# Shifted-window transformer block: the attention loop of the matmul engine regrouped, y finished in three parts, x loaded behind y's store

## The chip, the cores and the metric

The kernel runs on one core of a Trainium2 chip. The core has five engines with a program each: TensorE (PE, matmuls; PEld is its weight load), VectorE (DVE), ScalarE (ACT), GpSimd (POOL) and SyncE (SP), which here issues nearly all DMAs. They wait for one another by semaphores. The metric is the device time of one execution in microseconds (us), the median of several runs.

## The reference, cut to what matters

```python
x: (32, 56, 56, 128)   # windows 7 x 7, shift 3, 16 heads of 8, hidden 512
y   = roll(layernorm(x) * g1 + b1, (-3, -3))           # cut into 8 x 8 windows of 49 tokens
q, k, v = split(y @ qkv_w.T + qkv_b)
a   = softmax(q * 8 ** -0.5 @ k.T + rel_bias + mask)    # 49 x 49 for each window and head
o   = (a @ v) @ proj_w.T + proj_b
x1  = x + roll(o, (3, 3))
h   = gelu((layernorm(x1) * g2 + b2) @ fc1_w.T + fc1_b)
out = x1 + h @ fc2_w.T + fc2_b
```

## The kernel before

A step works on one band: seven image rows of two images, 16 windows in 8 pairs w = 0 to 7. There are 128 steps, and a software pipeline of turns t = -2 to 130 (`turns`, `body`): turn t runs the attention of step t, the row maxima of step t+1 (max_logits on PE, `row_maxima` on DVE), the projection and second norm of step t-1 and the two-layer perceptron (fc1, gelu, fc2) of step t-2, and loads x of step t+3. Each engine's program is written out in the order in which it runs; nothing is scheduled by a planner. PE, DVE and ACT are strictly in the order of the code, with semaphores between them.

In a turn PE first does the **front**: pv of the last window quartet of step t-1, `TZ` (transposes of z, L853), `TX` (of x, L861), the transpose of the maxima (L758), the rest of the fc2 rows of step t-3 (L832, L837), fc1 chunks 0 and 1 (L814), the q and k projections (L882), fc1 chunks 2 and 3, the spreading of the reciprocals of the softmax sums (L896), v (L910) and the output projection (L919). Then comes the **loop** over w. I call its pieces L (logits of a window pair, L780 and L785), M (max_logits, L750), P (pv of two window pairs, L800) and F (fc2 of one of seven rows i, 8 matmuls L832 and 4 L837). The loop before is L0 L1 M0 F M1 L2 P0 M2 L3 F M3 L4 P1 M4 L5 F M5 L6 P2 M6 L7 F M7, and P3 opens the next front. fc2 rows 3 to 6 are done in the loop (part 1 of `FC2_PARTS`), rows 0 to 2 in the front of the next turn (part 0).

What one piece waits for: M(w) waits until DVE has taken the maxima of M(w-1) (s_max), since both use banks 0 and 1. L(w) waits for the exp of w-2 on ACT (two pairs of banks), P(u) for the exps of its two pairs and for ACT's copy of P(u-1). fc2 writes bank 7. `finish` (L569, DVE) adds the scaled fc2 rows to x1_b and writes y_out; SP stores y_out when both parts are finished (s_fin). The F rows of a turn also need hid_hi (DVE, L578 and L580) and hid_lo (POOL, L375).

DVE in the loop takes the maxima of M(w) (L587) and in each gap some statistics: of x1 at w = 0 to 2, the aggregate (L512) at w = 3, of x_in of step t+3 (L506) at w = 4 to 6, after s_x says that it has landed. Behind the loop come `finish` of part 1 and the moments of x_in. In the front DVE does, in order: h_lo, neg_maxT, yT_lo, the reciprocal (L628), `finish` of part 0, hid_hi 0 and 1, k_lo and q_lo (L639), oT (L655), hid_hi 2 and 3, v, x. ACT does in the front h_hi, yT_hi, a table load, gelu 0 and 1 (L421), k_hi and q_hi (L467), gelu 2 and 3, a table load and copies of v; in the loop the exps (L406) and the copies of P (L414).

SP issues in a turn, in this order: sums out of pv_sb (L235), the load of x_in for step t+3 (L186), oT_raw (L248), the negated maxima (L224), r_rows (L261: the split reciprocals, for L896), mx_k and mx_q (L273, L277), the store of y_out (L186), fifteen copies for st_k and st_q (L292, L295) and the load of x_res (L186). The loads of x_in and x_res, the store and oT_raw are two DMAs of 196 KB each, r_rows two of 24.5 KB. Before it issues one it waits on its semaphores, and all that stands behind waits too.

Of the kernel before, what the change touches and what calls it, by code (L numbers as in the profile page):

```python
# [38 lines left out]
FC2_PARTS = ((0, 3), (3, 7))  # L39
# [10 lines left out]
def swin_block_kernel(nc, x, wqT, wkT, wvT, wvpT, wpT, w1T, w2T, cols, rows, table_k, table_q, ident, eye,  # L50
# [11 lines left out]
    with ctx:  # L62
# [134 lines left out]
        def _(sp):  # L197
# [29 lines left out]
            def body(t, edge, odd):  # L227
# [8 lines left out]
                n = t + 3  # L236
                if exists(n):

                    sp.wait_ge(s_st1, n)
                    if past(n, 1):  # L240
                        sp.wait_ge(s_t1, n - 1)
                    band_dmas(sp, xr, x_in[odd(3)], n, edge(n), False, s_x)
# [67 lines left out]
        def _(pool):  # L310
# [31 lines left out]
            def body(t, edge, odd):  # L342
# [22 lines left out]
                if exists(n):  # L365
                    if past(n, 0):
                        pool.wait_ge(s_fin, 2 * n)
# [20 lines left out]
        def _(act):  # L388
# [35 lines left out]
            def body(t, edge, odd):  # L424
# [59 lines left out]
                if exists(t):  # L484
                    for w in range(NW):
# [3 lines left out]
                        if w % 2 == 0 and w > 0:  # L489
                            copy_pv(t, w // 2 - 1)  # L490

# [4 lines left out]
        def _(dve):  # L496
# [64 lines left out]
            def finish(n, p, edge):  # L561

                i0, i1 = FC2_PARTS[p]
                if p == 1:
                    dve.wait_ge(s_x1b, n + 1)
                    if past(n, 0):
                        dve.wait_ge(s_stored, loads(n - 1, edge(n) and edge(n - 1)))
                dve.wait_ge(s_fc2, 2 * n + 2 - p)
                nc.vector.scalar_tensor_tensor(  # L569
                    y_out[:, i0:i1, :], ps[0:TP, 7, 0:(i1 - i0) * C].rearrange("p (i c) -> p i c", c=C),  # L570
                    1 / W_SCALE, x1_b[:, i0:i1, :], ALU.mult, ALU.add).then_inc(s_fin, 1)

            def hid_high(n, c):
                dve.wait_ge(s_gelu, CH * n + c + 1)
                if c == 0 and past(n, 0):
                    dve.wait_ge(s_fc2, 2 * n)
# [16 lines left out]
            def body(t, edge, odd):  # L593
# [35 lines left out]
                if exists(t - 3):  # L629
                    finish(t - 3, 0, edge)  # L630
# [54 lines left out]
                for w in range(NW):  # L685
# [3 lines left out]
                    if exists(n):  # L689
# [5 lines left out]
                        if w == 3:  # L695
                            aggregate(n, st2, s_st2, mv2, s_ln2)
                    n = t + 3
                    if exists(n):

                        if w == 4:  # L700
                            dve.wait_ge(s_x, loads(n, edge(n)))
                            stats(x_in[odd(3)], st1, (0, 1))
                        if w == 5:
                            stats(x_in[odd(3)], st1, (1, 4))
                        if w == 6:
                            stats(x_in[odd(3)], st1, (4, WS)).then_inc(s_st1, 1)
                if exists(t - 2):
                    finish(t - 2, 1, edge)
# [6 lines left out]
        def _(pe):  # L715
# [102 lines left out]
            def fc2(n, p, i):  # L818
                first, end = FC2_PARTS[p]
                if i == first and p == 1:  # L820
# [4 lines left out]
                    elif n > 0:  # L825
                        pe.wait_ge(s_fin, 2 * n)
                if i == first and p == 0:
                    pe.wait_ge(s_fin, 2 * n + 1)
                row = ps[0:TP, 7, (i - first) * C:(i - first + 1) * C]
# [4 lines left out]
                for c in range(CH):  # L834
                    if i == first and p == 1:
# [5 lines left out]
            def body(t, edge, odd):  # L841
# [30 lines left out]
                if exists(n):  # L872
                    pe.wait_ge(s_y_lo, n + 1)
                    high, low = ([y[odd(1)][:, :, im, 0:WT] for im in range(2)] for y in (yT_hi, yT_lo))
                    for w_hi, w_lo, bank in ((wk_hi, wk_lo, 0), (wq_hi, wq_lo, 6)):
                        if bank == 6 and exists(t):
                            pe.wait_ge(s_negT, t + 1)
                        if bank == 6 and exists(t - 3):
                            pe.wait_ge(s_fin, 2 * (t - 3) + 2)
# [20 lines left out]
                if exists(n):  # L900
                    if exists(t + 1):
                        pe.wait_ge(s_lo, 2 * (t + 2))
                    else:
                        pe.wait_ge(s_negT, t + 1)
                        if exists(t - 3):
                            pe.wait_ge(s_fin, 2 * (t - 3) + 2)
# [14 lines left out]
                for w in range(NW):  # L921
                    if exists(t):
                        if w != 1:
                            logits(t, w, edge, odd(0))
                        if w == 0:
                            logits(t, 1, edge, odd(0))
                        if w % 2 == 0 and w > 0:
                            pv(t, w // 2 - 1)
                    if exists(t - 2) and w % 2:
                        fc2(t - 2, 1, FC2_PARTS[1][0] + w // 2)  # L930
                    if exists(t + 1):
                        max_logits(t + 1, w, edge)
# [64 lines left out]
```

## Time and profile before

| | us |
|---|---|
| runs of the kernel before | 3899.22, 3900.76, 3903.62 (median 3900.76) |
| the profiled execution, its own time | 3904.86 |
| its span, first to last instruction | 3903.1 |
| PE busy in it | 3744.1 (96%) |
| DVE busy | 3087.1 (79%) |
| POOL busy | 2884.4 (74%) |
| ACT busy | 2776.0 (71%) |
| mean granted clock of TensorE, share of full speed | 0.993 |

The busy time of PE counts modelled ends of pipelined matmuls, so its idle time is best read between the starts of instructions. The span is divided by 128 steps: from one output projection (L919) to the next PE takes between 29.24 and some 30.6 us in the steady part, half of the turns below 29.42, 29.51 in the mean of 124 turns. Idle time of the other engines costs only where PE, or a chain that PE waits for, stands behind it.

### The profile page before, as it was taken

The page shows a single profiled execution, that of the slowest core. Times are in us where ns is not written, and L with a number is a line of the kernel's source. Part 1 is how long each engine was busy: PE and PEld are TensorE (multiplying, and loading weights), DVE is VectorE, ACT ScalarE, POOL GpSimd, SP SyncE. Part 2 cuts the span into 40 slices and gives each one's busy share as a digit, 9 for nine tenths or more (in the row PEclk, how much of TensorE's full clock was granted, in tenths as well). Part 3 has the DMA queues.
Part 4 walks back from the last instruction along what each step waited for, and adds up shares of the span by engine and source line. Part 5 has one row for each costly group of instructions (what it writes and reads, how often), then busy time and mean ns, then how long its engine had stood idle before and what let it go on. Part 6 is the DMA issues. An engine that isn't in the chain of part 4 may idle for free. (4 is left out here: it accounts for less than half of the span.)

```text
span 3903.1 us, 176619 instructions
## 1 busy us (share of the span) xinstructions
PE 3744.1 (96%) x75664; PEld 2946.8 (76%) x75664; DVE 3087.1 (79%) x7840; ACT 2776.0 (71%) x3840; POOL 2884.4 (74%) x3988
## 2 busy tenths in 40 slices
PE   2899999999999999999999999999999999999997
PEld 1677777777777777777777777777777777777776
DVE  6788878878878878878887888888888788888874
ACT  1677777777777777777777777777777777777774
POOL 5577777777777777777777777777777777777775
PEclk8999999999999999999999999999999999999999
DMA  2343334434434434433433344333344334333331
GB/s 76 106 119 118 115 112 118 119 111 116 121 114 115 118 115 118 117 115 115 118 117 111 115 119 116 114 117 116 111 118 120 112 116 119 115 115 117 117 108 58
DMA packets 603457, 441.97 MB, mean 113 GB/s; under 512 B 135939, under 2 KB 602227, under 8 KB 602675
## 3 DMA queue, kind: packets, MB, share of 16 engines
q1 hardware_dynamic: 602211, 428.86, 37.2%
q8 instruction: 597, 9.78, 1.1%
q14 instruction: 185, 1.52, 0.1%
q0 software_dynamic: 464, 1.81, 0.1%
HBM read 106.14 MB, written 51.46 MB: 40 GB/s over the span
## 5 line engine op out<-in xcount | busy, mean ns | idle before, releaser
L587 DVE TENSOR_REDUCE neg_max<-ps 113x16 f32<-113x784 f32 x1024 | 999.6, 976 | 545.5 <-PE ps L750 439.1
L406 ACT ACTIVATE probs<-ps 113x784 f32<-113x784 f32 x1024 | 848.1, 828 | 656.9 <-PE ps L785 539.5
L375 POOL TENSOR_TENSOR hid_lo<-probs,hid_hi 128x784 f16<-128x784 f32 x512 | 881.3, 1743 | 76.6 <-DVE hid_hi L580 76.3
L785 PE MATMUL ps<-st_q,st_k 128*49 128x196 f16 x8192 | 694.5, 249 | 0.0
L780 PE MATMUL ps<-bias,eye_k 106*64 106x392 f16 x4096 | 684.3, 331 | 0.0
L750 PE MATMUL ps<-mx_k,mx_q 128*49 128x196 f16 x8192 | 541.6, 253 | 60.3 <-DVE neg_max L587 52.4
L785 PEld LDWEIGHTS ps<-st_q,st_k 128*49 128x49 f16 x8192 | 440.2, 105 | 125.4 <-issue 0.5
L421 ACT ACTIVATE probs<-ps,col 128x784 f32<-128x784 f32 x512 | 467.6, 913 | 89.5 <-PE ps L814 60.1
L832 PE MATMUL ps<-w_hi,hid_hi 128*112 128x128 f16 x3584 | 521.7, 226 | 3.8 <-DVE hid_hi L580 3.0
L832 PE MATMUL ps<-w_lo,hid_hi 128*112 128x128 f16 x3584 | 498.8, 220 | 0.0
L832 PEld LDWEIGHTS ps<-w_hi,hid_hi 128*112 128x112 f16 x3584 | 417.7, 130 | 83.8 <-issue 79.4
L800 PE MATMUL ps<-probs,v_own 113*32 113x49 f32 x32768 | 470.3, 209 | 8.3 <-issue 7.6
L800 PEld LDWEIGHTS ps<-probs,v_own 113*32 113x32 f32 x32768 | 397.1, 110 | 92.3 <-issue 90.9
L750 PEld LDWEIGHTS ps<-mx_k,mx_q 128*49 128x49 f16 x8192 | 317.3, 103 | 137.6 <-DVE neg_max L587 74.4
L832 PEld LDWEIGHTS ps<-w_lo,hid_hi 128*112 128x112 f16 x3584 | 419.1, 131 | 0.0
L338 POOL TENSOR_SCALAR x_in<-x_in,rs,nm 112x128 f32<-112x128 f32 x896 | 389.4, 450 | 13.5 <-POOL nm L333 0.4
L338 POOL TENSOR_SCALAR z<-x,rs,nm 112x128 f32<-112x128 f32 x896 | 388.7, 450 | 13.5 <-POOL nm L333 0.4
L329 POOL TENSOR_TENSOR rs<-ve,half 112x7 f32<-112x7 f32 x256 | 380.4, 1486 | 21.3
L414 ACT ACTIVATE pv_sb<-ps 128x392 f32<-128x392 f32 x512 | 255.2, 498 | 182.0 <-PE ps L800 171.4
L356 POOL TENSOR_SCALAR r_hi<-sums 128x98 f16<-128x98 f32 x128 | 36.4, 284 | 461.3 <-DVE sums L628 461.3
L350 POOL TENSOR_TENSOR x_res<-x_res,proj_b 112x896 f32<-112x896 f32 x128 | 268.9, 2101 | 131.2 <-DMA x_res<-in_x 131.1
L837 PE MATMUL ps<-w_hi,hid_lo 128*112 128x128 f16 x3584 | 349.3, 220 | 3.4 <-POOL hid_lo L375 3.4
(119 smaller groups left out, 8009.9 us busy)
## 6 DMA issues: line engine op xcount, KB each, us to landing
st_k<-k_hi SPq DMA_DIRECT2D x256, 196.0 KB
st_q<-q_hi SPq DMA_DIRECT2D x1024, 49.0 KB
oT_raw<-pv_sb SPq DMA_DIRECT2D x256, 196.0 KB, 3.8
x_in<-in_x SPq DMA_DIRECT2D x224, 196.0 KB
x_res<-in_x SPq DMA_DIRECT2D x224, 196.0 KB
out_y<-y_out SPq DMA_DIRECT2D x224, 196.0 KB
mx_k<-k_hi SPq DMA_DIRECT2D x512, 49.0 KB
mx_q<-q_hi SPq DMA_DIRECT2D x128, 196.0 KB
```

The costliest lines, as they stand in the source:

```text
L329: nc.gpsimd.tensor_tensor(rs[:, :], ve[:, :], half[:, :], ALU.pow).then_inc(s_rs, 1)
L338: last = nc.gpsimd.tensor_scalar(z[:, i, :], src[:, i, :], rs[:, i:i + 1], nm[:, i:i + 1], ALU.mult, ALU.add)
L375: nc.gpsimd.tensor_tensor(hid_lo[:, c, :], hid[:, c, :], hid_hi[:, c, :], ALU.subtract).then_inc(s_hid_lo, 1)
L406: nc.scalar.activation(probs[0:KP, w % 4, :].rearrange("p (b c) -> p b c", b=2), ps[0:KP, b:b + 2, 0:HB * WT], ACT.Exp).then_inc(s_exp, 1)
L421: nc.scalar.activation(hid[:, c, :].rearrange("p (b q) -> p b q", b=2), ps[:, bank:bank + 2, 0:HT], ACT.Gelu, bias=col[:, BF + c:BF + c + ...
L587: nc.vector.tensor_reduce(neg_max[0:KP, :, :, w].rearrange("p e g -> p g e"), ps[0:KP, 0:2, :].rearrange("p b (g c) -> p (b g) c", g=2)[:, ...
L750: last = mm(group(im, 0, g, 256), mx_q[edge(n)][:, g, span], mx_k[:, g, :, span], start=True, stop=True)
L780: mm(ps[HP * im:HP * (im + 1), bank + b, 0:HB * WT], eye_k[0:BIAS_ROWS, kind, im, :], bias[0:BIAS_ROWS, b, :], start=True, stop=False)
L785: last = mm(group(im, bank, g, EQ * WT), st_k[par][:, g, span], st_q[par][:, :, g, span], start=False, stop=(g % 2 == 1))
L800: last = mm(ps[32 * r:32 * r + VC, 6, first:first + WT], v_own[0:KP, w, h, :], probs[0:KP, w % 4, h * WT:(h + 1) * WT], start=True, stop=True)
L832: mm(row, hid_hi[:, c, i * TP:(i + 1) * TP], w_part[:, c, :], start=(c == 0 and w_part is w2_hi), stop=False)
L837: last = mm(row, hid_lo[:, c, i * TP:(i + 1) * TP], w2_hi[:, c, :], start=False, stop=(c == CH - 1))
```

## The change

1. **fc2 rows.** `FC2_PARTS` becomes rows 0-1, 2-3 and 4-6. Five rows (0 to 4) are done in the loop and two (5 and 6) in the front. Part p may start when part p-1 is finished, for p > 0.
2. **The loop of PE** is written out: L0 L1 M0 F0 F1 M1 L2 P0 M2 L3 L4 M3 P1 L5 M4 F2 F3 M5 L6 L7 M6 P2 F4 M7. fc2 rows stand in twos at two places, and the logits L3 L4 and L6 L7 follow each other.
3. **finish** (DVE): parts 0 and 1 (two rows each) after the maxima of w = 3 and w = 5, part 2 (three rows) where part 0 stood in the front; the one behind the loop is gone. Of the statistics of x_in three rows stand at w = 4 and one at w = 5, where it was one and three.
4. **ACT** copies P2 behind the exp of w = 7, which was behind the exp of w = 6.
5. **SP** loads x_in behind the store of y_out.

```diff
-FC2_PARTS = ((0, 3), (3, 7))
+FC2_PARTS = ((0, 2), (2, 4), (4, 7))
+FC2_BANK = (0, 2, 0)
+PARTS = len(FC2_PARTS)
...
@@ block.sync: x_in (of step t+3) was issued ahead of oT_raw, now behind this @@
                 n = t - 3
                 if exists(n):
-                    sp.wait_ge(s_fin, 2 * (n + 1))
+                    sp.wait_ge(s_fin, PARTS * (n + 1))
                     band_dmas(sp, outr, y_out, n, edge(n), True, s_stored)
+                n = t + 3
+                if exists(n):
+
+                    sp.wait_ge(s_st1, n)
+                    if past(n, 1):
+                        sp.wait_ge(s_t1, n - 1)
+                    band_dmas(sp, xr, x_in[odd(3)], n, edge(n), False, s_x)
...
-                        if w % 2 == 0 and w > 0:
+                        if w in (2, 4):
                             copy_pv(t, w // 2 - 1)
+                    copy_pv(t, NU - 2)
...
@@ finish @@
-                if p == 1:
+                if p == 0:
...
-                dve.wait_ge(s_fc2, 2 * n + 2 - p)
+                dve.wait_ge(s_fc2, PARTS * n + p + 1)
...
@@ fc2 @@
-                if i == first and p == 0:
-                    pe.wait_ge(s_fin, 2 * n + 1)
+                if i == first and p > 0:
+                    pe.wait_ge(s_fin, PARTS * n + p)
...
@@ front of PE @@
                 if exists(t - 3):
-                    for i in range(*FC2_PARTS[0]):
-                        fc2(t - 3, 0, i)
+                    fc2(t - 3, 5)
+                    fc2(t - 3, 6)
```

In what follows, three places in the order of the instructions. On PE in the middle of the loop, before: F, M3, L4, P1, M4, L5 (L837 is the end of an fc2 row, L750 M, L780 and L785 L, L800 P).

```order
L837 MATMUL ps<-w_hi,hid_lo 112x128 x4
L750 MATMUL ps<-mx_k,mx_q 49x196 x8
L780 MATMUL ps<-bias,eye_k 64x392 x2
L785 MATMUL ps<-st_q,st_k 49x196 x4
L780 MATMUL ps<-bias,eye_k 64x392 x2
L785 MATMUL ps<-st_q,st_k 49x196 x4
L800 MATMUL ps<-probs,v_own 32x49 x32
L750 MATMUL ps<-mx_k,mx_q 49x196 x8
L780 MATMUL ps<-bias,eye_k 64x392 x2
L785 MATMUL ps<-st_q,st_k 49x196 x4
L780 MATMUL ps<-bias,eye_k 64x392 x2
L785 MATMUL ps<-st_q,st_k 49x196 x4
```

The same place in the changed kernel, where the lines are L756 for M, L786 and L791 for L and L806 for P: M2, L3 and L4, M3, P1.

```order
L756 MATMUL ps<-mx_k,mx_q 49x196 x8
L786 MATMUL ps<-bias,eye_k 64x392 x2
L791 MATMUL ps<-st_q,st_k 49x196 x4
L786 MATMUL ps<-bias,eye_k 64x392 x2
L791 MATMUL ps<-st_q,st_k 49x196 x4
L786 MATMUL ps<-bias,eye_k 64x392 x2
L791 MATMUL ps<-st_q,st_k 49x196 x4
L786 MATMUL ps<-bias,eye_k 64x392 x2
L791 MATMUL ps<-st_q,st_k 49x196 x4
L756 MATMUL ps<-mx_k,mx_q 49x196 x8
L806 MATMUL ps<-probs,v_own 32x49 x32
```

The fc2 row that stood between L3 and M3 is gone, and L4 has moved ahead of M3.

On DVE in the same loop, from the maxima of w = 3 (L587 is neg_max) to the moments behind the loop, before:

```order
L587 TENSOR_REDUCE neg_max<-ps 113x4x4
L512 BN_AGGR mv<-st 112x2 x7
L587 TENSOR_REDUCE neg_max<-ps 113x4x4
L506 BN_STATS st<-x_in 112x6
L587 TENSOR_REDUCE neg_max<-ps 113x4x4
L506 BN_STATS st<-x_in 112x6 x3
L587 TENSOR_REDUCE neg_max<-ps 113x4x4
L506 BN_STATS st<-x_in 112x6 x3
L587 TENSOR_REDUCE neg_max<-ps 113x4x4
L569 SCALAR_TENSOR_TENSOR y_out<-ps,x_b 112x512
L512 BN_AGGR mv<-st 112x2 x7
```

And now, where L591 is neg_max and L573 finish:

```order
L591 TENSOR_REDUCE neg_max<-ps 113x4x4
L515 BN_AGGR mv<-st 112x2 x7
L573 SCALAR_TENSOR_TENSOR y_out<-ps,x_b 112x256
L591 TENSOR_REDUCE neg_max<-ps 113x4x4
L509 BN_STATS st<-x_in 112x6 x3
L591 TENSOR_REDUCE neg_max<-ps 113x4x4
L573 SCALAR_TENSOR_TENSOR y_out<-ps,x_b 112x256
L509 BN_STATS st<-x_in 112x6
L591 TENSOR_REDUCE neg_max<-ps 113x4x4
L509 BN_STATS st<-x_in 112x6 x3
L591 TENSOR_REDUCE neg_max<-ps 113x4x4
L515 BN_AGGR mv<-st 112x2 x7
```

finish of four rows behind the loop has become two of two rows, after the maxima of w = 3 and of w = 5.

On SP, from the copy of the sums to the first st_k, before (L186 with x_in is the load of x, with out_y the store):

```order
L235 DMA sums<-pv_sb 128x1x49 x2
L186 DMA x_in<-in_x 56x7x128 x2
L248 DMA oT_raw<-pv_sb 128x1x392 x2
L224 DMA st_q<-neg_maxT 1x128x98
L261 DMA r_rows<-r_hi 16x8x98
L261 DMA r_rows<-r_lo 16x8x98
L273 DMA mx_k<-k_hi 8x4x784 x4
L277 DMA mx_q<-q_hi 32x4x784
L186 DMA out_y<-y_out 56x7x128 x2
L292 DMA st_k<-k_hi 32x4x784
```

And now (L188 for both):

```order
L237 DMA sums<-pv_sb 128x1x49 x2
L243 DMA oT_raw<-pv_sb 128x1x392 x2
L226 DMA st_q<-neg_maxT 1x128x98
L256 DMA r_rows<-r_hi 16x8x98
L256 DMA r_rows<-r_lo 16x8x98
L268 DMA mx_k<-k_hi 8x4x784 x4
L272 DMA mx_q<-q_hi 32x4x784
L188 DMA out_y<-y_out 56x7x128 x2
L188 DMA x_in<-in_x 56x7x128 x2
L294 DMA st_k<-k_hi 32x4x784
```

The load of x_in no longer stands ahead of oT_raw, the maxima and r_rows, but behind the store of y and ahead of the st copies and x_res.

## Rows read from the trace of the kernel before

**Rows 1.** Waits of PE: engine line <- releaser: us in total, times, longest us

```profile
PE ps L750 <- DVE neg_max L587: 52.4, 140, 1.1
...
PE ps L896 <- DMA r_rows<-r_lo: 8.1, 14, 1.9
```

**Rows 2.** PE in order of time, a loop: start us, duration us, engine line [idle before]

```profile
1743.49 0.36 PE L780 MATMUL ps<-bias,eye_k 106*64 106x392 f16 x2
...
1744.88 0.51 PE L750 MATMUL ps<-mx_k,mx_q 128*49 128x196 f16 x8
1745.32 0.26 PE L832 MATMUL ps<-w_hi,hid_hi 128*112 128x128 f16 x1
...
1746.52 0.53 PE L750 MATMUL ps<-mx_k,mx_q 128*49 128x196 f16 x8 [0.32 <-DVE neg_max L587]
...
1748.49 0.53 PE L750 MATMUL ps<-mx_k,mx_q 128*49 128x196 f16 x8
1748.86 0.33 PE L780 MATMUL ps<-bias,eye_k 106*64 106x392 f16 x2
...
1749.64 0.26 PE L832 MATMUL ps<-w_hi,hid_hi 128*112 128x128 f16 x1
...
1750.44 0.53 PE L750 MATMUL ps<-mx_k,mx_q 128*49 128x196 f16 x8
```

**Rows 3.** PE in order of time, the front that follows that loop

```profile
1758.29 0.53 PE L750 MATMUL ps<-mx_k,mx_q 128*49 128x196 f16 x8
1758.75 0.90 PE L800 MATMUL ps<-probs,v_own 113*32 113x49 f32 x64
1759.58 0.89 PE L853 MATMUL ps<-idn,z 112*128 112x112 f32 x7
...
1761.75 0.22 PE L832 MATMUL ps<-w_hi,hid_hi 128*112 128x128 f16 x1
...
1763.09 0.49 PE L814 MATMUL ps<-h_hi,w_hi 128*128 128x392 f16 x2
...
1769.21 0.50 PE L896 MATMUL ps<-r_rows,sel 32*128 32x392 f16 x2
1769.64 0.23 PE L910 MATMUL ps<-wv_hi,yT_hi 128*128 128x128 f16 x1
...
1771.02 1.24 PE L919 MATMUL ps<-w_p,oT 128*112 128x128 f32 x9
```

**Rows 4.** ACT in order of time, same turns: exp of w=3, gelu, k_hi

```profile
1749.80 0.82 ACT L406 ACTIVATE probs<-ps 113x784 f32<-113x784 f32 x1 [0.56 <-PE ps L785]
...
1764.29 1.91 ACT L421 ACTIVATE probs<-ps,col 128x784 f32<-128x784 f32 x2 [0.43 <-PE ps L814]
1766.38 0.93 ACT L467 ACTIVATE k_hi<-ps,col 128x784 f16<-128x784 f32 x1 [0.19 <-PE ps L882]
```

**Rows 5.** DVE in order of time, same turns: maxima of w=3, aggregate, finish, q_lo

```profile
1751.02 0.98 DVE L587 TENSOR_REDUCE neg_max<-ps 113x16 f32<-113x784 f32 x1 [0.39 <-PE ps L750]
1751.91 0.57 DVE L512 BATCH_NORM_AGGREGATE mv<-st 112x2 f32<-112x6 f32 x7
...
1764.23 0.49 DVE L569 SCALAR_TENSOR_TENSOR y_out<-ps,x_b 112x384 f32<-112x384 f32 x1
...
1768.42 1.15 DVE L639 SCALAR_TENSOR_TENSOR q_lo<-ps,col,q_hi 128x392 f16<-128x392 f32 x2
```

**Rows 6.** SP in order of time, same turns: DMA issues and their durations

```profile
1741.74 1.12 SPq L186 DMA_DIRECT2D out_y<-y_out  x2
...
1761.61 1.00 SPq L186 DMA_DIRECT2D x_in<-in_x  x2
...
1766.28 0.62 SPq L261 DMA_DIRECT2D r_rows<-r_lo  x1
```

**Rows 7.** DMAs of tile r_rows, whole run: us from issue to landing

```profile
DMA to landing us min/median/max: 2.0/2.5/3.4
```

**Rows 8.** The same, window 3770 to 3800 us, where no x is loaded

```profile
DMA to landing us min/median/max: 2.0/2.0/2.0
```

More of the change, by code:

```diff
@@ L629, in body @@
                 if exists(t - 3):
-                    finish(t - 3, 0, edge)
+                    finish(t - 3, 2, edge)
                 if exists(t - 2):
@@ L696, in body @@
                             aggregate(n, st2, s_st2, mv2, s_ln2)
+                    if exists(t - 2) and w == 3:
+                        finish(t - 2, 0, edge)
+                    if exists(t - 2) and w == 5:
+                        finish(t - 2, 1, edge)
                     n = t + 3
@@ L816, in fc1, with fc2 @@
                 last.then_inc(s_fc1, 1)
-            def fc2(n, p, i):
+            def fc2(n, i):
+                p = next(k for k, (first, end) in enumerate(FC2_PARTS) if first <= i < end)
                 first, end = FC2_PARTS[p]
-                if i == first and p == 1:
+                if i == 0:
                     pe.wait_ge(s_hid_hi, CH * (n + 1))
@@ L825, in fc2 @@
                     elif n > 0:
-                        pe.wait_ge(s_fin, 2 * n)
-                if i == first and p == 0:
-                    pe.wait_ge(s_fin, 2 * n + 1)
-                row = ps[0:TP, 7, (i - first) * C:(i - first + 1) * C]
+                        pe.wait_ge(s_fin, PARTS * n)
+                if i == first and p > 0:
+                    pe.wait_ge(s_fin, PARTS * n + p)
+                place = FC2_BANK[p] + i - first
+                row = ps[0:TP, 7, place * C:(place + 1) * C]
                 for c in range(CH):
@@ L834, in fc2 @@
                 for c in range(CH):
-                    if i == first and p == 1:
+                    if i == 0:
                         pe.wait_ge(s_hid_lo, CH * n + c + 1)
@@ L920, in body @@
                         last.then_inc(s_proj, 1)
[L921 to L932, printed above, removed]
+                now, mlp, ahead = exists(t), exists(t - 2), exists(t + 1)
+                if now:
+                    logits(t, 0, edge, odd(0))
+                    logits(t, 1, edge, odd(0))
+                if ahead:
+                    max_logits(t + 1, 0, edge)
+                if mlp:
+                    fc2(t - 2, 0)
+                    fc2(t - 2, 1)
+                if ahead:
+                    max_logits(t + 1, 1, edge)
+                if now:
+                    logits(t, 2, edge, odd(0))
+                    pv(t, 0)
+                if ahead:
+                    max_logits(t + 1, 2, edge)
+                if now:
+                    logits(t, 3, edge, odd(0))
+                    logits(t, 4, edge, odd(0))
+                if ahead:
+                    max_logits(t + 1, 3, edge)
+                if now:
+                    pv(t, 1)
+                    logits(t, 5, edge, odd(0))
+                if ahead:
+                    max_logits(t + 1, 4, edge)
+                if mlp:
+                    fc2(t - 2, 2)
+                    fc2(t - 2, 3)
+                if ahead:
+                    max_logits(t + 1, 5, edge)
+                if now:
+                    logits(t, 6, edge, odd(0))
+                    logits(t, 7, edge, odd(0))
+                if ahead:
+                    max_logits(t + 1, 6, edge)
+                if now:
+                    pv(t, 2)
+                if mlp:
+                    fc2(t - 2, 4)
+                if ahead:
+                    max_logits(t + 1, 7, edge)
             turns(body)
```

23 lines of the change are left out of this document (8 added, 15 removed).

## The prediction

> **What bounds the kernel now.** I read the busy shares first, then the waits, then one turn in order of time on each engine. TensorE (PE) is the engine that hardly stops; DVE, ACT and POOL wait for it more than it waits for them. So a turn costs what PE's pieces cost from start to start, plus its few waits. By name these are small: 52.4 us for M behind DVE's maxima, 8.1 us for the spreading of the reciprocals behind the DMA of r_rows [rows 1]. In the turn of [rows 2, 3] the first appears once, 0.32 us ahead of M1. From the first logits (1743.49) to P3 (1758.75) the loop takes 15.26 us, from TZ (1759.58) to the projection (1771.02) the front takes 11.44 us.
>
> Second, each piece costs more when its neighbour is of another kind. An fc2 row between strangers takes 0.80 us up to the next M (1749.64 to 1750.44), a row beside rows 0.67 (two rows from 1761.75 to 1763.09) [rows 2, 3]. M ahead of L takes 0.37 (1748.49 to 1748.86), ahead of F or P 0.44 to 0.46 (1744.88 to 1745.32; 1758.29 to 1758.75). L ahead of F takes 0.78, two L ahead of M together 1.39, so some 0.70 each. P takes 0.83 [rows 2, 3].
>
> Third, the front is a chain on several engines which PE only just does not wait for. The projection needs oT (DVE), that needs the spread reciprocals and q_lo; v needs q_lo, which ends at 1768.42 + 1.15 = 1769.57, and v starts at 1769.64 [rows 3, 5]. r_rows is issued at 1766.28, and the median landing is 2.5 us, so it is there at 1768.78, 0.43 ahead of the use at 1769.21 [rows 3, 6, 7]. Whatever PE saves here is worth only as much as these two give way.
>
> **Part 1, the loop.** The new loop in pieces: L0 L1 to M0 1.39; M0 0.44; F0 F1 0.67 + 0.80 = 1.47; M1 0.37; L2 0.78; P0 0.83; M2 0.37; L3 L4 1.39; M3 0.46; P1 0.83; L5 0.70; M4 0.46; F2 F3 1.47; M5 0.37; L6 L7 1.39; M6 0.46; P2 0.83; F4 0.80; M7 0.46. The sum is 15.27 us, against 15.26 now: the fifth fc2 row (0.67) comes in at no cost, because the stall ahead of M1 goes (0.4) and three fc2 groups instead of four change over (0.2). P ahead of L or F is not in the trace; P ahead of TZ is 0.83, I take that, and the dearest changeover seen, 0.14, is the upper bound: 2 x 0.14 a turn, 35 us for all. The lower one is nothing.
>
> Do new waits arise? M(w) can follow M(w-1) by what M1 does now, 1746.52 - 1744.88 = 1.64. The new distances are 1.91, 1.98, 1.76, 1.99, 1.93, 1.76, 2.09: all above. On DVE the widest slot is w = 3: the maxima start 0.58 after M3, the aggregate 0.89 later, it lasts 0.57, and then comes the new finish of two rows; three rows take 0.49 [rows 2, 5]. With 0.34 to 0.49 for two, y's first part is ready 2.4 to 2.55 us after M3, and F2, which now waits for it, is due 0.46 + 0.83 + 0.70 + 0.46 = 2.45 after M3. So 0 to 0.15 us; I take 0, since two rows must be shorter than three and an instruction starts a little before its forerunner's end (0.89 for 0.98). P1 needs the exp of w = 3: it starts 0.94 after L3 (1748.86, 1749.80) and lasts 0.82, so it ends 1.76 after L3, and P1 is due at 1.39 + 0.46 = 1.85 [rows 2, 4]. Copying P2 behind the exp of w = 7 costs nothing: P3 needs the copy 2.1 us after P2's start, where exp and copy are through. The finish that left the space behind the loop ends a piece of DVE time in which it then waits for ACT anyway: nothing gained.
>
> **Part 2, the front.** PE does two fc2 rows instead of three: 0.67 us less from TZ on. What of it arrives?
> - ACT waited 0.43 ahead of gelu and 0.19 ahead of k_hi, both for PE [rows 4]. With PE 0.67 earlier both waits vanish, and the chain gelu, k_hi, k_lo, q_lo comes 0.6 us earlier, no more, for then ACT is full. So v can start 0.6 earlier.
> - r_rows is needed at 1769.21 - 0.67 = 1768.54; at a landing time of 2.5 us it is late by 0.24.
>
> So I put the front at 0.60 less, if r_rows lands within 2.2 us.
>
> **Part 3, the move of x.** The load of x (196 KB twice) stands now between the sums and oT_raw on SP and takes its place in the rings ahead of r_rows (1761.61, r_rows 1766.28) [rows 6]. In the four last turns no x is loaded, with all else in place: there r_rows lands in 2.0 us each time, against 2.5 median and 3.4 at most over the run [rows 7, 8]. The new order is that of those turns. So r_rows is there at 1768.28, ahead of 1768.54. The waits of the tail, some 3 of the 8.1 us [rows 1], go too.
> What stands behind x on SP now comes about 1.0 us later (1.00 is its issue time): fifteen st copies, needed in the next turn only, and x_res, needed by POOL half a turn later; I price both at nothing. x itself is issued at about 1742.9 (behind the store of 1741.74 and 1.12) and is read behind the maxima of w = 4, some 3.5 us after M3 at 1750.44: 11 us for it [rows 2, 6].
> The Trainium skill says in "DMA: Bandwidth & Descriptors", section Rules for kernel authors, that a DMA should be issued early and waited for late. That rule speaks against moving x back by nearly half a turn. Its own result is the third rival below; no row here shows x being waited for in either place.
>
> **Sum.** A turn: loop +0.01, front -0.60, so -0.59; over 125 turns with all parts in them -74 us, with the tail of r_rows -77. The profiled execution took 3904.86 us, so it would take 3828; against the median of the runs, 3900.76, that is 3824.
> The changeover can be weighed against a page. In this trace it costs: 0.80 against 0.67 for F, 0.46 against 0.37 for M. The Trainium skill ("TensorE: Matmul & The Clock Gate", Part 2, step by step) says that PE pulls a weight load ahead of running matmuls when row groups do not conflict or the background buffer is free; by that a changeover would be hidden, and grouping would bring 0.4 for the stall alone and not 0.6, 25 us less. The measured rows decide for 0.6.
>
> **Rivals.**
> - **r_rows stays at 2.5 us**, since oT_raw (the same size as x, twice) is still ahead of it. For: oT_raw is issued earlier but as close. Against: [rows 8]. Then the front gives 0.67 - 0.24 = 0.43, with the spread to 3.4 about 0.40, and the turn 0.39: 49 us, 3852.
> - **A small new wait in the loop**: F2 behind finish by up to 0.15, or P1 behind exp, where only 0.09 is left. At 0.12 a turn 15 us are lost: 3839. For: both are near. Against: they are on the right side.
> - **x comes too late (slower)**: DVE stands at w = 4 in front of s_x, the maxima of w = 5 behind it, and M6 of PE behind these. It decides from a landing time of 11 us on, and becomes a loss over the whole once that is 11.7, for a turn has 0.6 to give. At 12.1 us the loss is 0.4 a turn: 50 us, 3950. For: store and load, 784 KB, now follow each other, with the st copies behind. Against: the longest landing time in the rows, that of the small r_rows, is 3.4 us; a large transfer would have to take over three times that.
> - **Nothing gained**: another operand of the front (h_lo for fc1, x for M0) is as late as it is now relative to P3, so that PE saves 0.67 and waits 0.6. Then 3899. For: the front is tight everywhere. Against: in the turn shown PE has no wait in it except changeovers, and ACT's waits for PE show that PE was the later one.
>
> **How the numbers follow.** Forecast 0.62 (3808 to 3834), r_rows 0.15, a small wait 0.14, x late 0.04, nothing gained 0.05. The likeliest gives 3824. The range, 3806 to 3856, holds the first three: below, 0.67 in the front and all waits behind DVE and r_rows gone (95 us); above, the r_rows case. Within 0.2% (7.8 us, about what a measurement of this kernel can tell from no change) only "nothing gained": 0.04, with 0.01 of it and the x case on the slow side. Faster 0.91, same 0.04, slower 0.05.
>
> **What the profile would show.** Right: M behind neg_max is under 10 us in the waits of PE; L0 to P3 takes 15.3 us with five fc2 rows in it, TZ to the projection 10.8; r_rows lands in 2.0 to 2.2 us. ACT's waits of 0.43 and 0.19 ahead of gelu and k_hi are close to 0, which is the sign that the front is at its end. Wrong would be: PE waiting at L904 for r_rows by more than 0.1 a turn (first rival), fc2 behind y_out or pv behind probs (second), DVE's statistics of x_in behind DMA (third).

## The result: 0.64% slower, and the profile after

| us | before | after |
|---|---|---|
| runs, same chip | 3899.22 to 3903.62, median 3901.45 (4) | 3924.51 to 3929.18, median 3925.34 (4) |
| ratio after to before | | 1.0064, 95% interval 1.0052 to 1.0077 |
| span of the profiled execution | 3903.1 | 3922.7 |
| mean granted clock | 0.993 | 0.994 |
| PE busy | 3744.1 (96%) | 3723.3 (95%) |
| DVE busy | 3087.1 (79%) | 3149.5 (80%) |

The prediction was 3824. PE did shed 21 us of modelled busy time, DVE gained 62, and the whole became longer. The second table cuts a turn of PE from projection to projection, mean start to start over the 122 to 124 turns in which every piece is recorded; the last column adds the waits of PE that the profile puts down to "issue", over the whole run. M0 is the first max_logits of a loop, P3 the last pv, SPR the spreading of the reciprocals, PR the projection.

| us a turn | PR, L0, L1 | M0 to P3 | P3 | TZ to SPR | SPR to PR | turn | "issue", us in all |
|---|---|---|---|---|---|---|---|
| before | 3.15 | 13.90 | 0.94 | 9.70 | 1.82 | 29.51 | 8.5 |
| after | 3.67 | 13.96 | 1.14 | 9.09 | 1.82 | 29.68 | 40.8 |

The front came out as forecast: 0.61 less from TZ on. The loop carries its fifth fc2 row at 0.06. What ate the gain stands in two columns: 0.52 ahead of M0 and 0.20 at P3. Together +0.17 a turn, 21 us over 124 turns, against 19.6 in the spans. The waits of PE in the changed kernel (engine line <- releaser: us in all, times, longest) name both, and answer to [rows 1]:

```profile
PE ps L756 <- DVE x L686: 47.8, 115, 0.6
PE ps L806 <- issue: 34.1, 42, 1.9
...
PE ps L756 <- DVE neg_max L591: 12.3, 13, 1.1
PE ps L904 <- DMA r_rows<-r_lo: 7.7, 16, 1.6
```

The same two waits before:

```profile
PE ps L800 <- issue: 7.6, 19, 1.1
...
PE ps L750 <- DVE x L682: 3.3, 8, 0.6
```

M behind the maxima fell from 52.4 to 12.3, a little above the 10 foreseen.

**Where the 0.6 went.** The end of the front in the kernel before, in order of time (start us, duration us, [idle before]): DVE, then POOL, then the start of M0 on PE. L655 is oT, L580 the pair of casts hid_hi 2 and 3, L682 the add that makes x; L375 is hid_lo, two and two.

```profile
1769.80 1.16 DVE L655 TENSOR_TENSOR oT<-oT_raw,ps 128x343 f32<-128x343 f32 x4 [0.23 <-issue]
1770.88 1.03 DVE L580 CAST hid_hi<-probs 128x784 f16<-128x784 f32 x2
1771.84 1.06 DVE L673 COPY v_own<-ps 49x512 f32<-49x512 f32 x1
1772.75 1.13 DVE L682 TENSOR_TENSOR x<-ps,x_res 112x512 f32<-112x512 f32 x2
...
1765.61 2.09 POOL L368 TENSOR_TENSOR x_b<-x,fc_b 112x896 f32<-112x896 f32 x1
1767.66 3.30 POOL L375 TENSOR_TENSOR hid_lo<-probs,hid_hi 128x784 f16<-128x784 f32 x2
...
1774.12 0.51 PE L750 MATMUL ps<-mx_k,mx_q 128*49 128x196 f16 x8
```

The same place in the changed kernel, a turn whose TZ starts at 2012.92 (before: 1759.58):

```profile
2022.47 1.17 DVE L659 TENSOR_TENSOR oT<-oT_raw,ps 128x343 f32<-128x343 f32 x4 [0.23 <-issue]
2023.55 1.66 DVE L584 CAST hid_hi<-probs 128x784 f16<-128x784 f32 x2
2025.14 1.09 DVE L677 COPY v_own<-ps 49x512 f32<-49x512 f32 x1
2026.07 1.14 DVE L686 TENSOR_TENSOR x<-ps,x_res 112x512 f32<-112x512 f32 x2
...
2018.96 2.09 POOL L370 TENSOR_TENSOR x_b<-x,fc_b 112x896 f32<-112x896 f32 x1
2021.01 3.31 POOL L377 TENSOR_TENSOR hid_lo<-probs,hid_hi 128x784 f16<-128x784 f32 x2
...
2027.36 0.53 PE L756 MATMUL ps<-mx_k,mx_q 128*49 128x196 f16 x8 [0.39 <-DVE x L686]
```

Count from TZ. oT starts at 10.22 before and at 9.55 now, the casts at 11.30 and 10.63: DVE's chain is 0.67 earlier, as said. POOL's x_b starts at 6.03 and 6.04: it hangs on the reciprocal (L628 at 1763.56, L632 at 2016.90: 3.98 after TZ both times), which stands ahead of the shortened fc2 rows and so gained nothing. POOL's first hid_lo pair ended at 1770.96, 0.08 after the casts began; now it ends at 2024.32, 0.77 after. And the casts take 1.66 us instead of 1.03. The 0.63 is what DVE had won: x starts at 13.17 and 13.15. PE is there 0.6 earlier and waits for it.

In both kernels the length of that pair of casts follows the time t for which POOL still runs after its start: 1.04 for t under 0.1 (106 turns of before), 1.66 for t about 0.8 (84 turns of after), 1.86 to 1.87 for t about 1.0 (4 turns of before, 25 of after). So it is about t + 0.9 from t = 0.2 on, as if the first cast waited for POOL's end. Nine turns of before, with t from 0.7 to 1.0, had already shown the price (1.59 to 1.87).

The Trainium skill has the rule, which I had not weighed: "SBUF — State Buffer", section Who interferes with whom, says that casts of DVE can take a pair of SBUF ports that GpSimd uses too, that whoever issues first holds it for the whole instruction while the other blocks, and that tensor_reduce on trn2 never takes it. The trace agrees on the cast (1.03 against 1.66); the reduce is tried below.

**Other lines of after.** ACT in the same turn, for [rows 4]: gelu 0 and 1 without a wait (0.43 before), k_hi at 6.14 after TZ (6.80 before) with the same 0.19.

```profile
2017.10 1.76 ACT L423 ACTIVATE probs<-ps,col 128x784 f32<-128x784 f32 x2
2019.06 0.93 ACT L469 ACTIVATE k_hi<-ps,col 128x784 f16<-128x784 f32 x1 [0.19 <-PE ps L890]
```

Landing of r_rows over the run, for [rows 7], which has 2.0/2.5/3.4 for the kernel before:

```profile
DMA to landing us min/median/max: 2.0/2.0/2.8
```

DVE behind the maxima of w = 3 in the loop ahead, for [rows 5]: finish of two rows takes 0.40.

```profile
2004.77 0.57 DVE L515 BATCH_NORM_AGGREGATE mv<-st 112x2 f32<-112x6 f32 x7
2005.25 0.40 DVE L573 SCALAR_TENSOR_TENSOR y_out<-ps,x_b 112x256 f32<-112x256 f32 x1
```

**The stalls in P3.** Of the 42 waits of L806 (pv) for "issue", 32 stand in P3, with 30.3 of the 34.1 us (18 and 7.2 us before). Five of them in a row of time (PE; x is how many of the 64 matmuls are left behind the gap, the bracket is the gap):

```profile
1213.57 0.39 PE L806 MATMUL ps<-probs,v_own 113*32 113x49 f32 x17 [1.52 <-issue]
1302.37 0.38 PE L806 MATMUL ps<-probs,v_own 113*32 113x49 f32 x16 [0.72 <-issue]
1391.71 0.38 PE L806 MATMUL ps<-probs,v_own 113*32 113x49 f32 x15 [1.24 <-issue]
1480.57 0.38 PE L806 MATMUL ps<-probs,v_own 113*32 113x49 f32 x14 [0.63 <-issue]
1569.69 0.37 PE L806 MATMUL ps<-probs,v_own 113*32 113x49 f32 x13 [1.23 <-issue]
```

They are 89 us apart, three turns, and each comes one matmul later in the program than the one before. Nothing that the program waits for moves like that. It is a place in the stream of instructions, at a distance of almost exactly three turns' worth, at which PE runs dry.

The trace shows what PE waits for there. Queue 8 carries instructions, here packets and MB of the changed kernel:

```profile
q8 instruction: 597, 9.78, 1.1%
```

Each of the 597 packets has 16384 bytes. PE has 152,864 instructions in the trace, matmuls, weight loads and semaphore waits together, so one packet stands for 256 of them (597 times 256 is 152,832). A turn has 1194; three turns are 3582, and 14 packets are 3584, two more (one matmul and its weight load). Counted from the first instruction, all 56 "issue" waits of PE in the changed kernel stand at place 193 to 195 of a block of 256, and PE goes on 1.2 to 1.7 us after a packet has ended. At its other blocks PE never passes this place sooner than 1.2 us after the packet. An example is the gap of 1.62 us in P3 that ends at 2280.84: the packet before it runs from 2278.01 to 2279.32. In the kernel before and the twelve experiments it is the same, place 193 to 195 and 1.1 to 1.8 us, for all of 396 waits but one in a set-up. So PE waits there for its own instructions. The Trainium skill ("Runtime: NRT & Kernel Launch", section Instruction fetch mechanics) says that an engine's instructions are refilled in blocks of 256, and the trace agrees; it calls the cost of a block's end mostly hidden, and with 34 us in pv here it isn't.

### The profile page after: what moved, and what is told of

It reads as the page before. It is cut to its first block and busy times, and to the rows that moved or that the text cites. A ratio compares the mean times of both kernels' runs of the same rounds, so it can differ in the third digit from the quotient of the medians.

```text
span 3922.7 us, 176747 instructions
## 1 busy us (share of the span) xinstructions
PE 3723.3 (95%) x75664; PEld 2953.5 (75%) x75664; DVE 3149.5 (80%) x7968; ACT 2741.3 (70%) x3840; POOL 2895.4 (74%) x3988
## 5 line engine op out<-in xcount | busy, mean ns | idle before, releaser
L591 DVE TENSOR_REDUCE neg_max<-ps 113x16 f32<-113x784 f32 x1024 | 1000.0, 977 | 464.7 <-PE ps L756 366.6
L408 ACT ACTIVATE probs<-ps 113x784 f32<-113x784 f32 x1024 | 822.0, 828 | 619.2 <-PE ps L791 400.9
L791 PE MATMUL ps<-st_q,st_k 128*49 128x196 f16 x8192 | 696.8, 249 | 2.1 <-issue 1.8
L786 PE MATMUL ps<-bias,eye_k 106*64 106x392 f16 x4096 | 688.3, 333 | 0.5 <-issue 0.3
L756 PE MATMUL ps<-mx_k,mx_q 128*49 128x196 f16 x8192 | 537.0, 251 | 66.3 <-DVE x L686 47.8
L791 PEld LDWEIGHTS ps<-st_q,st_k 128*49 128x49 f16 x8192 | 441.8, 105 | 128.6 <-issue 5.1
L806 PE MATMUL ps<-probs,v_own 113*32 113x49 f32 x32768 | 474.4, 209 | 34.9 <-issue 34.1
L806 PEld LDWEIGHTS ps<-probs,v_own 113*32 113x32 f32 x32768 | 398.3, 110 | 120.2 <-issue 78.6
L756 PEld LDWEIGHTS ps<-mx_k,mx_q 128*49 128x49 f16 x8192 | 338.1, 103 | 130.8 <-issue 68.4
```

The costliest lines, as they stand in the source:

```text
L408: nc.scalar.activation(probs[0:KP, w % 4, :].rearrange("p (b c) -> p b c", b=2), ps[0:KP, b:b + 2, 0:HB * WT], ACT.Exp).then_inc(s_exp, 1)
L591: nc.vector.tensor_reduce(neg_max[0:KP, :, :, w].rearrange("p e g -> p g e"), ps[0:KP, 0:2, :].rearrange("p b (g c) -> p (b g) c", g=2)[:, ...
L756: last = mm(group(im, 0, g, 256), mx_q[edge(n)][:, g, span], mx_k[:, g, :, span], start=True, stop=True)
L786: mm(ps[HP * im:HP * (im + 1), bank + b, 0:HB * WT], eye_k[0:BIAS_ROWS, kind, im, :], bias[0:BIAS_ROWS, b, :], start=True, stop=False)
L791: last = mm(group(im, bank, g, EQ * WT), st_k[par][:, g, span], st_q[par][:, :, g, span], start=False, stop=(g % 2 == 1))
L806: last = mm(ps[32 * r:32 * r + VC, 6, first:first + WT], v_own[0:KP, w, h, :], probs[0:KP, w % 4, h * WT:(h + 1) * WT], start=True, stop=True)
```

## The experiments

Theory A: the cast is held up by POOL's hid_lo, and through x delays M0. Theory B: PE's supply of instructions runs short in P3. The rival to both is that the move of x or the new loop is the cause by itself. All were compared with the kernel before on the same chip: 3900.61 us beside experiments 1 to 4, 3898.84 beside 5 to 8, 3903.45 beside 9 to 12, so that across these groups the ratios say more than the times. The figures of a turn and the stalls (waits of PE for "issue", in us over the run) are of the profiled execution.

### 1. x_b in two pieces, the first one earlier on POOL

Rows 0 to 3 of x_b are made between x_res and r_hi, rows 4 to 6 where all stood.

```diff
+                if exists(t - 2):
+                    x1_biased(t - 2, 0, 4)
+                if exists(n):
                     pool.wait_ge(s_rsum, n + 1)
...
-                    nc.gpsimd.tensor_tensor(x1_b[:, :, :], x1[:, :, :], ...
+                if exists(t - 2):
+                    x1_biased(t - 2, 4, WS)
```

> The changed kernel, but GpSimd's x1 + fc2_b (x_b, one instruction of 2.09 us behind r_lo) is split: rows 0 to 3 are done ahead of r_hi, where GpSimd idles 3.9 us, rows 4 to 6 in the old place. Same output. Theory A (shared resource): the cast of hid_hi 2 and 3 on DVE takes 1.66 us for the pair in the changed kernel and 1.04 before, because its first one runs while GpSimd's hid_lo 1 runs, and ends only after that. With hid_lo 1 some 1.2 us earlier the pair takes 1.04 again, x is 0.6 us earlier, M0's wait for x (0.5 us a turn, 115 turns) is gone: about 3925 - 60 = 3865 us. Rival A2 (DVE's cast is longer for a reason of its own place, for instance ACT's gelu beside it): the pair stays at 1.66 and the time within 10 us of the changed kernel's 3925. Stalls with releaser 'issue' in pv of the last quartet stay as they are (some 41 us) by either.

Measured: 3861.31, ratio 0.9903 (0.9884 to 0.9922), 64 us below the changed kernel. L584 of the changed kernel and L589 here (duration ns, min/median/max of one cast):

```profile
L584 DVE CAST hid_hi<-probs x256: 553/587/1925, 150.2 to 3905.4; 128x784 f16<-128x784 f32 x128
...
L589 DVE CAST hid_hi<-probs x256: 556/559/1922, 151.4 to 3844.1; 128x784 f16<-128x784 f32 x128
```

The pair is back at 1.04 in the median turn, PR to M0 at 3.14 and no wait for x among those of PE. So POOL's remaining work was the cause of the longer casts, and they of the wait. The edit costs something: behind the wait for x_res, POOL is late with r_hi in some turns, and PE waits for r_rows 26.7 us in 29 times (7.7 in 16 before the edit); TZ to SPR is 9.26 instead of 9.09. The stalls did not stay, as I had expected: they fell from 40.8 to 31.5, in pv from 34.1 to 19.5. So the 64 us are some 65 (0.53 a turn) ahead of M0 and some 15 at P3 and in the loop, less some 20 that the front lost.

### 2. x back in its old place

The load stands ahead of oT_raw again, and no longer behind the store.

```diff
+                band_dmas(sp, xr, x_in[odd(3)], n, edge(n), False, s_x)
...
-                band_dmas(sp, xr, x_in[odd(3)], n, edge(n), False, s_x)
```

> The changed kernel, with the load of x_in back in its old place on SP, between the sums and oT_raw; all else as changed. Theory B1 (the move of x is a gain or nothing): r_rows lands in 2.5 instead of 2.0 us again; PE waits for it in the front, but M0 waits for x of DVE less by the same amount, so the time is 3925 to 3940, and the 'issue' stalls in pv stay at 41 us. Rival B2 (the move of x is what hurts, since x_in, the st copies and x_res behind it then compete with the loading of instructions late in the turn): the 'issue' stalls fall from 41 to some 9 us as before, and the time falls to about 3895 to 3905.

Measured: 3892.75, ratio 0.9982 (0.9973 to 0.9991): in this company the move of x was a loss of 33 us. The front got longer, 9.23, since r_rows lands late again, but PE then waits less for x (3.47 ahead of M0), and the stalls fall from 40.8 to 20.0. That is neither B1, which had them at 41, nor B2, which had them at 9.

### 3. P2 between L6 and L7, as it stood before

```diff
                     logits(t, 6, edge, odd(0))
-                    logits(t, 7, edge, odd(0))
+                    pv(t, 2)
                 if ahead:
                     max_logits(t + 1, 6, edge)
                 if now:
-                    pv(t, 2)
+                    logits(t, 7, edge, odd(0))
```

> The changed kernel with the end of the loop as before: M5 L6 P2 M6 L7 F4 M7 (it was L6 L7 M6 P2 F4 M7), and ACT's copy of P2 behind exp 6 again. Theory C (two pv blocks, the densest in instructions, 64 + 64 in 0.83 us, stand only 2.1 us apart instead of 3.2, and the instruction supply of PE runs dry in the second): the 'issue' stalls in the last pv fall from 41 to some 10 us, and the time by 25 to 30 us, to about 3897. Rival C2 (the stalls depend on where in the stream the supply's steps fall, not on the distance): they stay within 10 us of 41 and the time within 10 us of 3925.

Measured: 3902.41, ratio 1.0004 (0.9995 to 1.0014). Stalls 9.2, P3 0.91, wait for x as large as in the changed kernel (49.7 us in 120 times). The order of three pieces at the end of the loop is worth 23 us. M0 to P3 takes 0.09 more: that is what the grouping of L6 L7 had saved. By the packets of queue 8 this is a race. In the changed kernel, where a block's place 193 falls into P3, the 255 instructions ahead of it take 3.11 us in the median, and the packet ends 2.08 us after their start in the mean, so that with the 1.2 us at least behind its end PE can go on after 3.3. With P2 early they take 3.53, and the packet ends after 1.91: 3.1.

### 4. The stream of PE shifted by 64 matmuls

```diff
+            for _ in range(64):
+                mm(ps[0:HP, 5, 0:HP], eye_k[:, 0, 0, :], eye_k[:, 0, 0, :], start=True, stop=True)
             pe.wait_ge(s_inita, 2)
```

> The changed kernel with 64 small fp16 matmuls (128 instructions with their weight loads) more in the set-up, where PE waits for DVE anyway; they write a bank that is overwritten later and add nothing to the result. All that follows on PE is the same, but 128 instructions later in its stream. Theory C2: the stalls come every third turn at one place of the stream, since a step of the supply falls into the last pv of every third turn; shifted by 128 instructions the steps fall elsewhere, and the 'issue' stalls in the last pv fall to below 15 us, total time about 3900, or other places stall. Theory C (distance alone): stalls and time as in the changed kernel, 41 us and 3925.

Measured: 3913.48, ratio 1.0042 (1.0025 to 1.0059). The stalls are 34.7 (beside one of 11.2 in the set-up), in pv 22.9 instead of 34.1. Neither forecast came: the phase took a third of the stalls in pv and some 12 us, and did not remove them. With hindsight it can't. The stall's place moves through pv by one matmul in three turns, and pv with its weight loads is 128 instructions. A turn is 4 2/3 blocks of 256, so in any three turns the places 193 lie a third of a block (some 85 instructions) apart, and one always falls into P3, wherever the count starts.

### 5. The kernel before, with x behind the store

The edit is that of experiment 2, the other way round and in the kernel before.

> The kernel before with the one edit of SP: the load of x_in stands behind the store of y_out. Theory B2 (the move makes the supply of PE's instructions late in the last pv): the 'issue' stalls rise from 8.5 us to 20 or more, the waits for r_rows fall by 5 us at most, and the time rises by 5 to 20 us, to 3906 to 3920. Theory B1 (the move hurts only in the new loop, where the two last pv stand close together): the stalls stay at about 9 us and the time within 0.2% of 3900.6, or 3 to 7 us under it.

Measured: 3894.39, ratio 0.9988 (0.9978 to 0.9997). The move alone gives 4 to 5 us, by the waits for r_rows (8.1 to 4.2 us) and fewer stalls (3.2). In the kernel before, r_rows at 2.5 us was not the last thing that PE waited for.

### 6. x_b in two pieces, rows 0 to 3 first of all on POOL

As experiment 1, with the first piece ahead of x_res.

```diff
             def body(t, edge, odd):
+                if exists(t - 2):
+                    x1_biased(t - 2, 0, 4)
```

> As the first experiment (x_b split, rows 0 to 3 early), but these rows stand ahead of GpSimd's x_res + proj_b, where it waits for the DMA of x_res, and not behind it. In the first experiment GpSimd was then late for r_hi in 39 of 128 turns, and the stretch from the transposes to L909 took 9.26 us, against 9.09. Theory: that is r_lo's lateness; here the stretch is 9.09 again and 0.17 x 123 = 20 us go: 3842 us. Rival: r_rows is late for another reason (x_res's DMA itself): within 7 us of 3861.

Measured: 3844.15, ratio 0.9857 (0.9843 to 0.9872): 17 us better than experiment 1, TZ to SPR 9.12, PR to M0 3.13. That was the cost noted there. The earlier x_b is worth about 80 us in the changed kernel, 67 of them (0.54 a turn) ahead of M0. P3 is still long, with stalls of 35.2 us.

### 7. Experiment 6 with P2 early

> The former with the end of the loop as before the change (P2 between L6 and L7, its copy behind exp 6). Theory C: the stalls 'issue' fall to 10 us from about 30; the loop costs 0.1 a turn more by its changeovers: 3842 - 20 + 12 = about 3834 us. Rival: with shorter turns the supply of instructions is late at other places, the stalls stay at 30 us: 3842 to 3855.

Measured: 3822.72, ratio 0.9805 (0.9790 to 0.9819). The waits of PE, whose first three rows are those of the start of the program and not shown:

```profile
PE ps L759 <- DVE neg_max L594: 12.6, 13, 1.1
PE ps L907 <- DMA r_rows<-r_lo: 8.5, 16, 1.7
```

Stalls 5.4, PR to M0 3.13, turn 28.84. It came out 11 us under the 3834 expected, since the stalls fell by 30 us and not by 20. This is the fastest kernel of the study, 2% below the one before. That it lies 1.3 us from the time predicted for the change alone is in part luck: against before, the front gives 0.68 a turn and not 0.60, the loop costs 0.12 and not 0.01, and P3 gives 0.08.

### 8. Experiment 7 with x in its old place

> The former with the load of x_in in its old place as well. Theory B1: with the stalls gone the move of x is a gain, since r_rows lands in 2.0 us with it and in 2.5 without, and now nothing else hides that: here the wait for r_rows is back, 0.2 to 0.25 a turn: 3860 us, slower than the former by 25 to 30. Theory B2: the move costs on its own; here the time is 15 to 30 us under the former.

Measured: 3849.90, ratio 0.9870 (0.9854 to 0.9886). With casts and P2 mended, the move of x is worth 27 us:

```profile
PE ps L907 <- DMA r_rows<-r_lo: 28.9, 61, 1.7
...
DMA to landing us min/median/max: 2.0/2.5/3.0
```

Here is the gain that the prediction's part 3 spoke of. In the changed kernel it was there too (r_rows 7.7 us, landing 2.0), but what PE won in the front it lost again ahead of M0.

### 9. hid_hi 2 and 3 by tensor_reduce

```diff
-                if c < 2:
+                if True:
                     last = nc.vector.tensor_reduce(hid_hi[:, c, :], hid[:, c, :].unsqueeze(2), AX_X, ALU.max)
```

> Edit: in the changed kernel DVE makes hid_hi 2 and 3 by tensor_reduce too, as it makes 0 and 1, where it was tensor_copy. Same work, same place in the order. Theory (only the copy is held up by POOL): the pair of reduces lasts about 1.94 us whatever POOL does, against 1.66 for the copies in the changed kernel; M0's wait behind x grows by 0.28 a turn, and the time becomes about 3925 + 35 = 3960. The mark is the pair's duration: the same within 0.05 us in every turn. Rival (whatever DVE runs beside POOL's hid_lo is held up, the kind of instruction does not matter): the reduces last 1.94 + 0.6 = 2.5 us and the time is about 4000 or more.

Measured: 3934.03, ratio 1.0084 (1.0069 to 1.0099), 9 us above the changed kernel. The pair, with POOL's hid_lo beside it in the same turn:

```profile
2030.93 1.84 DVE L582 TENSOR_REDUCE hid_hi<-probs 128x784 f16<-128x784 f32 x2
...
2028.37 3.31 POOL L377 TENSOR_TENSOR hid_lo<-probs,hid_hi 128x784 f16<-128x784 f32 x2
```

POOL runs 0.75 past the start of the reduces, and they last 1.84. Over the run 123 pairs have POOL running 0.3 us or more past their start and 133 have not: both groups go from 1.83 to 1.97, median 1.84. So it is the kind of instruction that matters, as "SBUF — State Buffer" in the Trainium skill says of tensor_reduce, and the rival is out. I had the size wrong: the pair is 0.18 longer than the held-up casts, not 0.28, for which the expectation counted two single reduces without their overlap. PR to M0 grew by 0.17, 21 us, of which 4 came back in smaller stalls and some in the loop.

### 10. Experiment 6 with x in its old place

> Edit: the changed kernel with x_b in two pieces (the piece of the first four rows first on POOL in the turn) and x loaded in its old place, but with P2 late as in the changed kernel. It fills the last corner of x place by P2 place. If the place of x and the place of P2 act apart from each other on the stalls ahead of the last pv, then from 3844 (x late, P2 late), 3823 (x late, P2 early), 3850 (x old, P2 early) it follows 3850 + 21 = 3871. If P2 late and x late are worse together than the sum (what the halved stalls of the second experiment say), it is faster than that: 3850 to 3858, with some 20 us of stalls ahead of the last pv.

Measured: 3862.45, ratio 0.9892 (0.9878 to 0.9907). The ratios to before of the four corners:

| | x behind the store | x in its old place |
|---|---|---|
| P2 late | 0.9857 | 0.9892 |
| P2 early | 0.9805 | 0.9870 |

The move of x is worth 0.65% with P2 early and 0.35% with P2 late. The additive forecast, 3871, is a ratio of 0.9929 by the 3898.84 beside which it was made, and lies above the interval; the other one, 3850 to 3858, is 0.9875 to 0.9895 and lies in it. So the two are worse together than their sum, by some 12 us, though the noise of four ratios, 0.15% each, can make as much. The stalls say it more clearly (in pv they are 20.4, as the second forecast has them): 35.2 with both late, 5.4 and 24.5 with one of them (x, P2), 13.3 with neither, where adding up would give 16.6 with both late.

### 11. The kernel before with x_b in two pieces and x late

> Edit: the kernel before, with x loaded behind y's store and with x_b in two pieces, the freer piece first on POOL. A control for the claim that the copy pair of DVE matters only because the front of PE became shorter. Theory: before, x (the operand of M0) is there when PE is, so POOL's x_b buys nothing: 3894, the time of the x move alone, within 0.2%. Rival (the split of x_b is worth its 64 to 81 us by itself, and the changed kernel has no part in it): 3894 - 70 = 3825.

Measured: 3887.42, ratio 0.9963 (0.9949 to 0.9977). Against experiment 5, the same without x_b, it is 0.25% or 10 us better, where I expected nothing and the rival 70. M0 comes 0.05 a turn earlier (3.10 against 3.15), 6 us, for the few waits behind x that the kernel before had; the remaining 4 us are within the noise. The split of x_b is worth 64 to 81 us where the front of PE is shortened, and 10 where it isn't.

### 12. P2 between L7 and M6

```diff
                     logits(t, 7, edge, odd(0))
+                    pv(t, 2)
                 if ahead:
                     max_logits(t + 1, 6, edge)
-                if now:
-                    pv(t, 2)
```

> Edit: the changed kernel with P2 between L7 and M6 instead of between M6 and F4; the copy of P2 on ACT stays where it is. From P2's start to P3's there are then 0.83 + 0.46 + 0.80 + 0.46 = 2.55 us instead of 2.1 (late) and 3.1 (P2 between L6 and L7). Theory (PE's supply of instructions is short where two pieces of 64 small matmuls lie close together): the stalls ahead of the last pv lie between 34 us (late) and 9 us (early), at about 20, and the time at 3925 - 14 = 3911. Rival (the stalls hang on something else near P3, such as M6 or F4 at that place of the stream): 30 us or more remain, and the time stays within 5 us of 3925.

Measured: 3943.17, ratio 1.0101 (1.0086 to 1.0116), slower than both expectations, by a mistake of mine that the waits show:

```profile
PE ps L756 <- DVE x L686: 50.3, 120, 0.6
PE ps L756 <- DVE neg_max L591: 47.4, 138, 1.1
PE ps L806 <- issue: 7.5, 14, 1.2
```

Only F4 lies between M6 and M7 then, 0.46 + 0.81 = 1.27 us, and M can follow M by 1.64 only. F4 with the wait behind it takes 1.14 instead of 0.81. So its time says nothing on the stalls. For theory B the run is still of use, with the distance that came out instead of the planned 2.55. From P2's start to P3's, and the "issue" waits of pv:

| | distance, us | waits of pv, us (times) |
|---|---|---|
| after | 2.10 | 34.1 (42) |
| 12, P2 between L7 and M6 | 2.89 | 7.5 (14) |
| 3, P2 between L6 and L7 | 3.24 | 6.6 (11) |
| before | 3.25 | 7.6 (19) |

The shorter the stretch in which PE has two pieces of 64 small matmuls to get through, the more it runs dry. Between 2.1 and 2.9 us the stalls nearly go. Distance isn't all: with the same loop and x in its old place (experiment 2) they are 17.0. There the packets for P3 end 0.35 us earlier in the mean (1.73 instead of 2.08). Why the late x delays them stays open. With P2 early it is the other way round: experiment 7 has x late and stalls of 5.4 us, experiment 8 has it early and 13.3.

## Why the prediction was wrong, point by point

- **Part 1, the loop: right.** Forecast +0.01 a turn, measured +0.06 from M0 to P3, and M1's wait is gone. Finish of two rows took 0.40, inside the 0.34 to 0.49 assumed; F2 waited for it 2.3 us in the whole run. P1's exp was in time (0.7 us). The rival of a small new wait in the loop did not come.
- **Part 1, its last step: wrong by omission.** The pieces were added up by their durations and by data they wait for. P2 late was costed at its copy only. The waits of before had pv behind "issue", 7.6 us in 19 times, and I left it out of [rows 1] as small. It became 34.1, and all stalls together +32.2 us. The prediction had no term for it.
- **Part 2, PE and ACT: right in size, not in its reason.** The front is 0.61 shorter against 0.60, and ACT's wait ahead of gelu is gone. But the cap of 0.6 was put down to ACT being full, and in the turn shown ACT still waits 0.19 ahead of k_hi, while k_hi comes 0.66 and oT 0.67 earlier. That 0.61 met 0.60 is partly luck; the front of experiment 7 gave 0.68.
- **Part 2, "the chain gelu, k_hi, k_lo, q_lo comes 0.6 us earlier": right up to v, and wrong for what follows.** I let all of DVE's chain move with PE and asked only whether v and the projection would find q_lo and oT. Behind oT stand the casts, v, x, and M0 waits for x. POOL's half of the front doesn't move, since it hangs on a reciprocal ahead of the shortened rows. The moved casts met POOL's unmoved hid_lo, and grew from 1.03 to 1.66. This is the step that failed; it cost 0.52 a turn, 64 us, and experiments 1, 6 and 9 show it.
- **Part 3, r_rows: right in itself.** Landing 2.0, waits 7.7 us (8.1 before, so little of the tail went). DVE waited for x_in once, 2.2 us at the start, so the "slower" rival was the wrong one. Its worth is 27 us where the rest lets it through (experiments 7 and 8) and minus 33 in the changed kernel (experiment 2).
- **"Nothing gained"** named the right operand, x for M0, and I gave it 0.05 since "in the turn shown PE has no wait in it". It has none there because x came 0.2 us ahead of its need, and I never asked by how much. The true outcome was that rival plus the stalls, 26 us beyond it.

Sum of the predicted -0.59: the front gave -0.61, the loop +0.06, x at M0 +0.52, P3 +0.20: +0.17. With both added terms mended (experiment 7) the turn is 28.84, against the 28.92 forecast.

## What to carry to other kernels

When one engine's work moves earlier, list for each other engine what its own start hangs on. What hangs on something ahead of the shortened part stays where it is, and pieces that used to pass each other can now meet. A cast of DVE beside a running GpSimd instruction is such a meeting, and the rare turns in which the trace already shows them together give its price before the change is made. A wait for "issue" is not noise if it comes at a fixed interval: here it said that many short instructions lay too close together, and spreading them by a piece of another kind took most of it away. The packets of the queue that carries instructions, beside the gaps, tell whether it is the supply.

## What the hardware showed that I had not expected

- A pair of casts (128x784, f32 to f16) of DVE takes 1.04 us alone and about t + 0.9 when POOL's tensor_tensor runs on for t after its start. A pair of tensor_reduce on the same data takes 1.84 with and without it.
- PE can run dry of instructions in a dense stretch: gaps of up to 1.86 us, every 89 us (three turns), each one matmul later in the program, 41 us of a 3923 us run, with no engine and no data behind them. Each gap of the changed kernel ends 1.2 to 1.7 us after a packet of 16384 bytes of the instruction queue, at one place of PE's blocks of 256. A shift of the program by 64 matmuls leaves 35 us, a wider spacing of the dense pieces nearly removes them (5 to 11 us).
- The same move of a DMA was worth -5, -14, -27 and +33 us in four surroundings (experiments 5, 10 to 6, 8 to 7, 2 to the changed kernel).
